# Routed experts 2 to 14: the first half's rows gathered whole, moved on chip in 32x128 squares and turned by VectorE

## What is computed

```python
buf = jnp.zeros((E, CAP, D), xt.dtype).at[e, posc].add(x_pairs)   # E = 16, CAP = 256, D = 512
g = jnp.einsum('ecd,eid->eci', buf, W1)                           # inner width 352
u = jnp.einsum('ecd,eid->eci', buf, W3)
h = jax.nn.silu(g) * u
out = jnp.einsum('eci,edi->ecd', h, W2)
y_pairs = out[e, posc] * (w.reshape(-1) * valid)[:, None]
y = y_pairs.reshape(T, K, D).sum(axis=1)
...
return (y + shared).astype(x.dtype).reshape(shape)
x = x + jnp.tanh(g_ffn[0]) * _L0_ffn_ref(_layernorm(x, axis=-1), ...)
```

## Time and profile before

| | |
|---|---|
| median of 3 runs | 471.63 us (471.3 to 471.88) |
| the profiled execution | 472.29 us, of it 470.3 us from the first to the last instruction (the span) |
| granted TensorE clock, mean over the span | 0.997 |
| TensorE busy | 453.3 us, 96% of the span |
| VectorE busy | 327.3 us, 70% |
| ScalarE busy | 267.3 us, 57% |
| GpSimd busy | 236.6 us, 50% |
| DMA | 31483 packets, 95.33 MB, mean 203 GB/s |

### The profile page before, as it was taken

How to read it: one execution, slowest core, us unless ns; L and a number is a source line. 1 busy time by engine, 2 the same in 40 slices (tenths; PEclk the granted TensorE clock), 3 DMA queues, 4 the chain that set the end, 5 groups by cost and what they waited for, 6 DMA issues and landing times.

```text
span 470.3 us, 7799 instructions
## 1 busy us (share of the span) xinstructions
PE 453.3 (96%) x2463; PEld 389.2 (83%) x2463; DVE 327.3 (70%) x731; ACT 267.3 (57%) x415; POOL 236.6 (50%) x196
## 2 busy tenths in 40 slices
PE   1999999999999999999999999999999999999995
PEld 1577888888888788888888989999999999999994
DVE  6698988888876654488559676766767666676342
ACT  5656666666654643643436576566566766666441
POOL 2704445654453465436177737475726848443453
PEclk9999999999999999999999999999999999999998
DMA  8524876887654542354289999998869998998464
GB/s 302 179 101 125 269 242 204 271 285 258 230 201 156 172 139 86 78 68 50 43 208 178 290 282 281 285 277 264 253 226 242 270 273 250 275 279 245 57 124 90
DMA packets 31483, 95.33 MB, mean 203 GB/s; under 512 B 5984, under 2 KB 8032, under 8 KB 30944
## 3 DMA queue, kind: packets, MB, share of 16 engines
q0 software_dynamic: 17344, 43.92, 38.2%
q1 hardware_dynamic: 13824, 51.05, 32.0%
q10 hardware_dynamic: 288, 0.01, 0.0%
HBM read 67.80 MB, written 28.74 MB: 205 GB/s over the span
## 4 chain that ended last, share of the span: by engine, by line
PE 80%; DVE 8%; DMA 7%; issue 2%; ACT 2%; POOL 1%; POOLq 0%; SPq 0%; ACTq 0%; DVEq 0%
PE psG L1485 43%; PE psY L1485 28%; PE psT L1490 5%; DMA raw<-in_w 2%; DMA xh_sb<-in_ctx_t 2%; PE psG L1758 1%; DMA front<-padded,idxc 1%; DMA ys<-in_x,idx 1%; DVE qhot L1390 1%; DVE slot L1217 1%; PE psT L1695 1%; DMA tok_i<-in_ids 1%; DVE xh_sb L1067 0%; POOL front L485 0%; DVE big L985 0%
## 5 line engine op out<-in xcount | busy, mean ns | idle before, releaser
L1485 PE MATMUL psY<-arena 128*128 (+1 forms) x366 | 89.3, 394 | 0.7 <-DVE arena L1079 0.7
L1485 PEld LDWEIGHTS psY<-arena 128*128 128x128 f32 x366 | 67.7, 188 | 14.9 <-issue 1.1
L1485 PE MATMUL psY<-slot,arena 128*128 128x512 f32 x240 | 59.0, 394 | 0.0
L1217 DVE TENSOR_TENSOR slot<-raw,slot 128x1536 fp32r<-128x1536 f32 x25 | 44.0, 1763 | 15.9 <-ACT slot L733 15.8
L1485 PE MATMUL psG<-arena 128*128 x216 | 53.9, 398 | 0.0
L1217 DVE TENSOR_TENSOR arena<-raw,arena 128x1536 fp32r<-128x1536 f32 x24 | 42.0, 1757 | 16.0 <-ACT arena L733 16.0
L1485 PEld LDWEIGHTS psY<-slot,arena 128*128 128x128 f32 x240 | 44.3, 188 | 9.2 <-ACT xh_sb L777 0.4
L1485 PE MATMUL psG<-arena,slot 128*128 128x512 f32 x216 | 51.4, 393 | 0.0
L586 POOL DMA_INDIRECT out<-ys,idx x16 | 31.0, 1940 | 35.0 <-DMA out<-xb,idx 26.4
L1485 PEld LDWEIGHTS psG<-arena,slot 128*128 128x128 f32 x216 | 40.1, 188 | 8.2
L1485 PEld LDWEIGHTS psG<-arena 128*128 128x128 f32 x216 | 39.2, 188 | 7.5
(11 more groups left out here) (256 smaller groups left out, 851.0 us busy)
## 6 DMA issues: line engine op xcount, KB each, us to landing
raw<-in_w SPq DMA_DIRECT2D x48, 768.0 KB, 5.8
padded<-xh_sb SPq DMA_DIRECT2D x19, 256.0 KB, 2.0
raw<-in_w SPq DMA_DIRECT2D x12, 192.0 KB, 3.2
raw<-in_ctx_t SPq DMA_DIRECT2D x2, 1024.0 KB, 7.9
ht<-in_ctx_t SPq DMA_DIRECT2D x1, 1024.0 KB, 10.9
xh_sb<-in_ctx_t SPq DMA_DIRECT2D x1, 1024.0 KB, 7.5
out<-log_sb SPq DMA_DIRECT2D x4, 256.0 KB, 3.1
ht<-out,idx POOLq DMA_INDIRECT x51, 4.9
```

The lines of the kernel that those rows point to most:

```text
L1217: dve.tensor_tensor(piece(SLOT[r][1], c), raw[:, c, :], as_f32(piece(SLOT[r][0], c)), ALU.subtract).then_inc(w_lo[c], 1)
L1485: ins = pe.matmul(ps, left[a], right[b], start=n == 0 and m == 0, stop=n == total - 1 and m == 2)
```

## The change

`TURNED` becomes the experts 2 to 14. No quarter gathers are left: every half is gathered whole into `ht`. For an expert in `TURNED`, SyncE then moves the first half's rows on chip: sixteen DMAs of 32 partitions by 128 values (16 KB each), the square in row block b and column block q of `ht` going to row block q and column block b of one of two further buffers, `moved_rows[r]`. VectorE's turn reads that buffer. SyncE issues the sixteen between `load(e, 2)` and `load(e + 2, 0)`, after a wait for the gather's landing and one for the turn of two experts before; its loop now handles two experts per pass. VectorE's turn waits for the squares and stands between the second `gate_rest` and `gate_first`, no longer at the head of the step. The quarter indices, their two VectorE operations, SyncE's write of them and its four reads go. The seven experts new in `TURNED` (2, 4, ..., 14) get the other weight order and the strided transpose of their second half.

```diff
-TURNED = range(3, E2 - 2, 2)
+TURNED = range(2, E2 - 1)
...
+        moved_rows = [big_all[:, 3 * NJ * E2:5 * NJ * E2], arena[:, 2 * SW:2 * SW + D].bitcast(F32)]
...
-            return known in TURNED if known is not None else r == 1
+            return known in TURNED if known is not None else True
...
-            sp.wait_ge(quarters_made, 1)
-            sp.dma_start(slot_quarters, idx_q[:, :, :].rearrange("p q e -> p (q e)")).then_inc(quarters_sent, 16)
-            sp.wait_ge(quarters_sent, 16)
-            for q in range(KD):
-                sp.dma_start(idx4[q * QP:(q + 1) * QP, :, :],
-                             slot_quarters[:, q * E2:(q + 1) * E2].rearrange("(b t) e -> t b e", b=KD)).then_inc(quarters_here, 16)
             for c in range(2):
                 load(2, c)
             load(3, 0)
-            with sp.Fori(2, E2 - 1) as s:
-                load(sp.snap(s + 1), 1)
-                load(s, 2)
-                load(sp.snap(s + 2), 0)
+            def move_squares(e, r, known):
+
+                if known == TURNED[1]:
+                    sp.wait_ge(up_ps, len(SEQ))
+                elif known != TURNED[0]:
+                    sp.wait_ge(g_ps[0], e - 1 if known is not None else sp.snap(e - 1))
+                sp.wait_ge(g_here[2 * r], landed(e, r))
+                for b in range(KD):
+                    for q in range(KD):
+                        sp.dma_start(moved_rows[r][q * QP:(q + 1) * QP, b * P:(b + 1) * P],
+                                     ht[b * QP:(b + 1) * QP, 2 * r, q * P:(q + 1) * P]).then_inc(moved[r], 16)
+
+            def load_and_move(e, r, known):
+                load(e + 1 if known is not None else sp.snap(e + 1), 1)
+                load(e, 2)
+                move_squares(e, r, known)
+                load(e + 2 if known is not None else sp.snap(e + 2), 0)
+
+            load_and_move(2, 0, 2)
+            load_and_move(3, 1, 3)
+            with sp.Fori(2, E2 // 2 - 1) as i:
+                load_and_move(sp.snap(i * 2), 0, None)
+                load_and_move(sp.snap(i * 2 + 1), 1, None)
+            load_and_move(E2 - 2, 0, E2 - 2)
...
-                    if e in TURNED and a == 0:
-                        pool.wait_ge(quarters_here, 16 * KD)
-                        for b in range(KD):
-                            pool.indirect_dma_start(ht[:, n, b * P:(b + 1) * P], None, quarters_of_out,
...
-                    else:
-                        pool.indirect_dma_start(ht[:, n, :], None, halves_of_out, slots(e * NA + a, 0)).then_inc(g_here[n], 16)
+                    pool.indirect_dma_start(ht[:, n, :], None, halves_of_out, slots(e * NA + a, 0)).then_inc(g_here[n], 16)
...
-            def turn(e):
-
-                dve.wait_ge(g_here[2], e * 32 - 16)
+            def turn(e, r):
+
+                dve.wait_ge(moved[r], (e - r) * 8 * KD * KD)
                 dve.wait_ge(g_lo, (e - 1) * NA + 1)
-                dve.transpose(psT[0][:, :], ht[:, 2, :].rearrange("p (b i k) -> p k b i", b=KD, k=KD)).then_inc(g_ps[0], 1)
+                dve.transpose(psT[0][:, :], moved_rows[r].rearrange("p (b i k) -> p k b i", b=KD, k=KD)).then_inc(g_ps[0], 1)
...
             def step(e, r, known):
-                if turns(e + 1, 1 - r, None if known is None else known + 1):
-                    turn(e + 1)
                 split(e + 2, 1, r)
                 gate_rest(e, r, known, 0)
                 split(e + 1, 2, 1 - r)
                 gate_rest(e, r, known, 1)
+                if turns(e + 1, 1 - r, None if known is None else known + 1):
+                    turn(e + 1, 1 - r)
                 gate_first(e, r, known)
```

More of the change, by code:

```diff
@@ L92, in gated_layer @@
         halves_of_out = out.rearrange("t (h d) -> (t h) d", h=2)
-        quarters_of_out = out.rearrange("t (g d) -> (t g) d", g=2 * KD)
-        slot_quarters = nc.dram_tensor("slot_quarters", (P, KD * E2), I32).ap()
         padded = nc.dram_tensor("padded", (NT * P, D), F32).ap()
@@ L166, in gated_layer @@
         w_slot = sb("w_slot", [P, NQ])
-        idx_f = sb("idx_f", [P, E2])
-        idx_q = sb("idx_q", [P, KD, E2], I32)
-        idx4 = sb("idx4", [P, KD, E2], I32)
         cur = sb("cur", [P, 8], I32)
@@ L279, in gated_layer @@
         g_ps = [sem(f"g_ps{a}") for a in range(NA)]
-        quarters_made, quarters_sent, quarters_here = (
-            sem(n) for n in ("quarters_made", "quarters_sent", "quarters_here"))
+        moved = [sem(f"moved{r}") for r in range(2)]
         up3_ps, silu3, hid3, hid3_hi, hid3_lo = (sem(n) for n in ("up3_ps", "silu3", "hid3", "hid3_hi", "hid3_lo"))
@@ L569, in gather @@
                         pool.wait_ge(g_ps[a], e - 1)
-                    if e in TURNED and a == 0:
-                        pool.wait_ge(quarters_here, 16 * KD)
-                        for b in range(KD):
-                            pool.indirect_dma_start(ht[:, n, b * P:(b + 1) * P], None, quarters_of_out,
-                                                    bass.IndirectOffsetOnAxis(ap=idx4[:, b, e:e + 1], axis=0)
-                                                    ).then_inc(g_here[n], 16)
-                    else:
-                        pool.indirect_dma_start(ht[:, n, :], None, halves_of_out, slots(e * NA + a, 0)).then_inc(g_here[n], 16)
+                    pool.indirect_dma_start(ht[:, n, :], None, halves_of_out, slots(e * NA + a, 0)).then_inc(g_here[n], 16)
             def add(e):
@@ L1355, in _ @@
             dve.scalar_tensor_tensor(idx2[:, :, 1], U[1], -1.0, U[2], ALU.add, ALU.add).then_inc(r2_idx, 1)
-            first_half = [u.rearrange("p (e a) -> p a e", a=NA)[:, 0] for u in (U[0], U[1])]
-            link(dve.scalar_tensor_tensor(idx_f[:, :], first_half[0], -2.0 * PAD, first_half[1], ALU.mult, ALU.add))
-            dve.scalar_tensor_tensor(idx_q[:, :, :], along(idx_f[:, :], KD), float(KD), over(iota[:, 0:KD], E2),
-                                     ALU.mult, ALU.add).then_inc(quarters_made, 1)
             hidden(10)
@@ L1701, in gathered @@
                     n = 2 * r + a
-                    if known == E2 - 1 and a == 0:
-                        pe.wait_ge(g_here[n], 16 * (KD * len(TURNED) + 2))
-                    else:
-                        pe.wait_ge(g_here[n], landed(e, r))
+                    pe.wait_ge(g_here[n], landed(e, r))
                     if known != 0:
```

## The result

The changed kernel takes **476.03 us** (median of 4 runs, 474.93 to 477.01) against 471.47 for the kernel before beside it: 1.0099 of its time, with a 95% interval of 1.0083 to 1.0116. The forecast was 469.3, with a range of 468.6 to 472.5. It was wrong, and in the sign. The profiled execution of after took 477.01 us, 475.1 of it span, at a granted clock of 0.996: 4.8 us of span more than before. In all that follows a time is the median of all of a kernel's executions and a ratio compares the fast ones alone, those no more than 1.5% above its fastest: left out are 1 of 7 in e_tiny, 2 of 10 in e_idle, 1 of 10 in g_after_drains, 3 of 9 in e_mix_drain (478 to 479 us) and 6 of 10 in e_quart (478 to 483 us), in e_tiny, e_idle and e_mix_drain with the profiled one among them.

A forecast was written before the change was run, and what follows sets the result against it. The prediction took TensorE, busy 96% of the span, to bound the kernel from 274.67 us on. Six long steps shedding 0.39 us each gave -2.34 us, the rest 0: 469.3 us from a median of 471.63, range 468.6 to 472.5.

The forecast's parts named there:

- What TensorE sheds: TensorE's six long steps: four strided transposes replace eight plain ones, 0.39 us less each, a gain of 2.34 us.
- The VectorE turn: Seven added turns of 1.11 us ahead of gate_first fit VectorE's idle of about 1.9 us: cost 0.
- The gathers: On GpSimd, one whole gather replaces four quarter gathers in six experts; GpSimd is half idle: 0.
- The squares on SyncE: Sixteen issues of 0.44 us, 7.0 us, fit the 7.3 us gap between load(e,2) and load(e+2,0): cost 0.
- The squares on the DMA engines: 512 rows per expert at 29 ns take 0.93 us of all engines per step, share 0.96: cost 0.
- rival A: DMA engines become the bound as squares delay load(e+2,0) in each step; 474 us, chance 0.12.
- The start: First weight loads, with gathers and squares competing: -0.7 to +0.4 us.
- Rival B: Squares on SyncE go one after another, each issue held until the one before landed; 594 us, chance 0.04.
- Rival C: Loads or moved rows late in some steps, most likely 1 to 3, hand back the gain; 471.6 us, chance 0.10.

The follow-up runs named there:

- e_tiny: Changed kernel with the same sixteen issues per expert, each moving only 4 of 128 values a row (16 bytes): 474.83 us, 1.0075 of the kernel before.
- e_idle: Changed kernel, its sixteen issues copying on-chip constants to a buffer nobody reads, VectorE's turn reading rows as gathered: 476.52 us, 1.0083 of the kernel before.
- g_after_drains: Changed kernel with GpSimd's drains behind add(0) and add(12) instead of add(4) and add(12): 473.3 us, 1.0032 of the kernel before.
- e_mix_drain: Changed kernel, odd experts by quarter gathers, even by squares, GpSimd's drains behind add(3) and add(11): 474.28 us, 1.0023 of the kernel before.
- e_quart: Kernel before with experts 2 to 14 all turned by VectorE from quarter gathers, no squares: 478.97 us, ratio 0.999.
- e_none: Changed kernel without squares, VectorE's turn reading the rows as gathered: 469.32 us, 0.9954 of the kernel before.
- e_mix: Changed kernel with odd experts by quarter gathers and even ones by squares: 478.5 us, 1.0175 of the kernel before.
- e_four: Changed kernel moving the same 512 rows per expert in four straight copies of 128x128, rows not rearranged: 468.94 us, 0.9953 of the kernel before.
- e_eight: Changed kernel moving the same 512 rows per expert in eight straight copies of 64x128: 469.94 us, 0.9974 of the kernel before.
- e_dram: Changed kernel, its sixteen issues copying from memory to a buffer nobody reads, turn reading rows as gathered: 471.66 us, 1.0007 of the kernel before.
- e_spread: Changed kernel with eleven squares ahead of load(e + 2, 0) and five behind it: 481.77 us, 1.022 of the kernel before.

## Why the prediction was wrong, point by point

- **What TensorE sheds** (2.34 us): right. e_none gives 2.2 us, six steps of 0.37 less each, and the new steps have 0.49 us of strided transposes.
- **The VectorE turn** (0): right, by e_none, and its wait for moved rows in after did no harm of its own: e_idle, where it does not wait for them, lost as much.
- **The gathers** (0): right for GpSimd's time, but incomplete. The prediction let a gather come later "but its squares go out more than a step after it". e_mix shows the other side: a gather held up by a drain makes squares late by as much, and the turn stood 5.42 us.
- **The squares on SyncE** (0): this step failed, twice. The price: 0.44 us was taken from four index loads, which read memory; squares read the chip's own memory and cost 0.63 to 0.70. The cover: the limit of 0.76 us a square was worked out for `load(e + 2, 0)` alone, and the price measured lies below it. The loads queued behind it were left out. Before, the three loads of a step go out 2 to 7 us apart; behind sixteen squares they go out, in the steps of the five waits, within 1.3 to 1.5 us, and the third, `load(e + 1, 2)`, lands last. In step 4 it lands 6 us later in its step than before; 3.2 us of that were ScalarE's cover and 1.8 what the gated rows had to spare (in before they were done at 311.72 and wanted at 313.50), and TensorE stood for the rest, 0.92 us. All five waits, 5.5 us, go back to this third load. The prediction found a cover of 2.3 us for one such load, `load(3, 2)`, and weighed it only against a DMA delay of 0.93 us. And as SyncE needs 11.9 to 12.7 of a step's 12.8 us, it makes up less than 1 us of a delay in the next step.
- **The squares on the DMA engines** (0; 29 ns a row, share 0.96): near. e_four's share of 0.98 against e_none's 0.90 is 0.08 x 138 us x 16 engines over 10.8 steps of 512 rows, an estimate of some 32 ns each from shares of two digits, with its share of the extra packets. DMA engines at 0.98 did not stop TensorE; rival A's mechanism is not what happened, and that its time, 474, is nearest to the result is luck. A row moved on the chip so cost what the neighbours in size made it, some 32 ns between the 17 and 52 of the earlier trace rows. (The 144 packets of the earlier trace rows are 128 rows and sixteen of the packets that each issue brings besides, so the 17 ns is a mean of both.)
- **The start** (-0.7 to +0.4): -1.4 in the profiled execution. It says little: the control with moved drains, the kernel before up to that point, reached it at 272.6, and e_none at 274.06.
- **Rival B** (issues one after another): not so; in e_four the moves went out 0.70 us apart while each, by the page, landed 7.0 us after its issue, so they were in flight together. But its place, "decides from 0.76 us a square", was the right place to look, with the wrong limit.
- **Rival C** (late loads in some steps) named what TensorE would wait for, but put it down to the DMA engines, at 471.6. None of the cases let SyncE be the bound by its issues alone, and none had the chain of adds, which the forecast left out as GpSimd is half idle: an engine half idle can still hold a chain of landings that is nearly as long as the step, and in before that chain had 0.35 us to spare at the end.

## What to carry to other kernels

A queue that issues transfers is an engine with a busy time: count all its issues per step, at the price of the same form from the same place, against the step's length, before asking what the DMA engines do. If the sum comes close to the step (here 93 to 99% of it), delays are no longer made up. And the cover that counts is that of the last transfer queued behind an insertion, not of the first alone; a row merging several issues ("x3") hides just that one. Last, before shortening what the path runs through, look how much the next chain has to spare at the end of the kernel.

## What the runs showed of the hardware that had not been expected

- A DMA issue of SyncE took 0.59 us at the median and 0.04 of gap when its source was on the chip and had 32 partitions, the same for 16 bytes (e_tiny) and 512 bytes a row (after); 0.60 with 64 partitions (e_eight) and 0.61 to 0.64 with 128 (e_four); 0.49 to 0.54 with its gap in a run of sixteen from memory (e_dram); 0.33 for a single 768 KB load.
- Small moves behind a 768 KB load in one queue went behind it. In e_spread the turn waited 2.6 us on the mean of thirteen (33.7 us) for the five squares so placed. All five were issued by 342.3, behind the load of 338.83, but from 339 to 342.4 the DMA engines started only packets of the load, which are of 6 KB, and none of the squares', which are of 512 bytes:

```profile
DMA packets 108, 0.66 MB, mean 195 GB/s; under 512 B 0, under 2 KB 0, under 8 KB 108
```

- After an idle of 2.34 us TensorE's granted clock fell in e_mix, and 24 products took 6.59 us that take 5.04 a step on. From 383.36 to 385.00 the granted clock is 0.50, the lower of the two levels of 1.2 and 2.4 GHz. The table by stretch has 0.90 for the stretch with the idle, which mixes the two, and 1.00 on either side:

```profile
363.00:376.00 13.00, 13.00 (x78) 11.90 (x77) 8.47 (x10) 8.27 (x12) 7.84 (x6) 1.00 0.83 211
376.00:393.00 17.00, 14.66 (x77) 12.99 (x77) 9.50 (x12) 8.47 (x13) 9.16 (x9) 0.90 0.86 288
393.00:406.00 13.00, 13.00 (x78) 11.87 (x77) 9.91 (x13) 8.53 (x13) 10.87 (x8) 1.00 0.79 221
```
